# Fp4 feed-forward stage: moving VectorE's first gating product ahead of the rounding of the previous gated tile

## The reference, cut to what matters

```
x = x + ffn(layernorm(x))
gate = fp4_linear(n, w_gate);  up = fp4_linear(n, w_up)     # 256 -> 704
h = silu(gate) * up
out = fp4_linear(h, w_down)                                 # 704 -> 256
fp4_linear(a, w): both a and w are rounded to a 4-bit grid, block by block of 16,
                  with scale = max|block| / 6 and 1/scale applied before the rounding
```

## Time and profile before

| | |
|---|---|
| median of 3 runs | 2474.6 us (2470.22 to 2474.79) |
| profiled execution, its own time | 2467.79 us |
| its span, first to last instruction | 2466.0 us |
| mean granted TensorE clock | 0.976 of full speed |
| PE busy | 2354.4 us, 95% |
| DVE busy | 1782.3 us, 72% |
| ACT busy | 1293.4 us, 52% |
| POOL busy | 702.0 us, 28% |
| fp4 stage in the span | from about 380 to 886 us |

### The profile page before, as it was taken

The page is one execution under the profiler, slowest core; times in us unless marked ns, Lnnn a source line. Parts: engine busy times, 40 slices in busy tenths (PEclk is TensorE's granted clock), DMA queues, the critical chain, the costliest instruction groups (busy, mean ns, idle before and its releaser), DMA issues.

```text
span 2466.0 us, 43761 instructions
## 1 busy us (share of the span) xinstructions
PE 2354.4 (95%) x16024; PEld 2179.2 (88%) x16024; DVE 1782.3 (72%) x3323; ACT 1293.4 (52%) x2027; POOL 702.0 (28%) x468
## 2 busy tenths in 40 slices
PE   7999997999999969999999999998999999999999
PEld 6999996999999958898898898987988998899998
DVE  5776777999999857557467566555887877877774
ACT  4445444444444326456456455455666665666554
POOL 1110112555444422312213123033334442311110
PEclk9999998999999989999999999987999999999999
DMA  5000000000000000000000000011000010000001
GB/s 185 0 0 0 0 1 20 1 0 0 0 0 1 1 18 1 18 9 9 17 9 9 17 9 9 17 48 48 18 26 17 17 51 29 9 24 20 26 26 35
DMA packets 43258, 45.68 MB, mean 19 GB/s; under 512 B 3120, under 2 KB 41904, under 8 KB 43184
## 3 DMA queue, kind: packets, MB, share of 16 engines
q1 hardware_dynamic: 43184, 44.69, 5.5%
HBM read 27.90 MB, written 16.78 MB: 18 GB/s over the span
## 4 chain that ended last, share of the span: by engine, by line
PE 53%; DVE 5%; issue 3%; ACT 2%; POOL 1%; DVEq 0%; ACTq 0%; POOLq 0%
PE m_ps_z L1891 13%; PE p_ps_a L1673 5%; PE p_ps_feat L279 4%; PE p_ps_a L1730 4%; PE p_ps_feat L281 3%; PE p_ps_feat L280 3%; PE m_ps_wide L279 3%; PE m_ps_wide L281 3%; PE m_ps_wide L280 3%; PE p_ps_a L1611 2%; PE p_ps_turn L1717 2%; PE m_ps_wide L1869 1%; PE m_ps_n L1852 1%; PE m_ps_wide L1870 1%; PE m_ps_z L1897 1%
## 5 line engine op out<-in xcount | busy, mean ns | idle before, releaser
L1983 DVE TENSOR_TENSOR m_a_lo<-m_a,m_a_hi 128x512 fp32r<-128x512 f32 x256 | 202.1, 806 | 144.1 <-ACT m_a_hi L1943 140.4
L1891 PE MATMUL m_ps_z<-m_w_hi,m_a_hi 128*128 128x256 f32 x1024 | 290.7, 284 | 1.6 <-DVE m_a_lo L1983 0.9
L1891 PE MATMUL m_ps_z<-m_w_hi,m_a_lo 128*128 128x256 f32 x1024 | 288.0, 281 | 0.0
L1891 PEld LDWEIGHTS m_ps_z<-m_w_hi,m_a_hi 128*128 128x128 f32 x1024 | 192.3, 188 | 13.6 <-DVE d_w_lo L2500 1.9
L1891 PEld LDWEIGHTS m_ps_z<-m_w_hi,m_a_lo 128*128 128x128 f32 x1024 | 192.7, 188 | 0.0
L1939 ACT ACTIVATE m_a<-m_ps_wide,d_b,d_w_gain 128x512 f32<-128x512 f32 x128 | 100.0, 781 | 135.5 <-PE m_ps_wide L281 131.4
L1356 POOL TENSOR_TENSOR p_kf<-p_kf,p_k_shift 128x1024 f32<-128x1024 f32 x64 | 119.5, 1905 | 155.4 <-DVE p_k_shift L1491 155.4
L1891 PE MATMUL m_ps_z<-d_w_lo,m_a_hi 128*128 128x256 f32 x512 | 144.7, 283 | 0.0
L1891 PE MATMUL m_ps_z<-m_w_lo,m_a_hi 128*128 128x256 f32 x512 | 143.6, 280 | 0.0
L1673 PE MATMUL p_ps_a<-p_ctx_pair,p_kf 128*128 128x34 f32 x1024 | 130.0, 285 | 0.0
L1673 PEld LDWEIGHTS p_ps_a<-p_ctx_pair,p_kf 128*128 128x128 f32 x1024 | 129.5, 205 | 0.4
(11 more groups left out here) (371 smaller groups left out, 8106.2 us busy)
## 6 DMA issues: line engine op xcount, KB each, us to landing
residual<-in_x SPq DMA_DIRECT2D x8, 1024.0 KB, 11.8
attn<-p_attn SPq DMA_DIRECT2D x32, 256.0 KB, 2.1
m_attn<-attn SPq DMA_DIRECT2D x16, 512.0 KB, 3.8
out<-residual SPq DMA_DIRECT2D x16, 512.0 KB, 2.9
raw_weights<-in_d_q SPq DMA_DIRECT2D x2, 1024.0 KB, 7.1
m_attn<-in_d_scale SPq DMA_DIRECT2D x3, 512.0 KB, 4.3
raw_weights<-in_m_w1T SPq DMA_DIRECT2D x1, 1024.0 KB, 4.8
raw_weights<-in_m_w2T SPq DMA_DIRECT2D x1, 1024.0 KB, 7.9
```

The lines of the kernel that those rows point to most:

```text
L1891: mm = pe.matmul(z, a, w[:, f, :], start=(f == 0 and k == 0 and j % 2 == 0), stop=(f == FC - 1 and k == 2), skip_group_check=True)
L1983: dve.tensor_tensor(self.a2[1][:, f, :], self.a[f % RING][:, :], self.a2[0][:, f, :].bitcast(F32), ALU.subtract).then_inc(self.a_lo, 1)
```

## The change

In VectorE's order of a step, `multiply(0)` of pair s - 5 stands ahead of `round_h` of pair s - 6 and no longer behind it. Both are DVE phases; nothing is added or removed, no other engine's order changes, and the orders of steps 5 and 6 stay as they are (step 6 already has `multiply(0)` ahead of `round_h`).

```diff
-            pipeline(dve, N, [(8, add_down), (4, split_n), (7, split_h(0)), (3, round_n), (6, round_h), (5, multiply(0)),
+            pipeline(dve, N, [(8, add_down), (4, split_n), (7, split_h(0)), (3, round_n), (5, multiply(0)), (6, round_h),
                               (7, split_h(1)), (2, scales_n), (5, multiply(1)), (5, scales_h)], SLOTS,
                      fill={5: [(4, split_n), (3, round_n), (5, lambda t, s: last_statistics()), (5, multiply(0)), (2, scales_n),
                                (5, multiply(1)), (5, scales_h)],
                            6: [(4, split_n), (3, round_n), (5, multiply(0)), (6, round_h), (2, scales_n), (5, multiply(1)), (5, scales_h)]},
```

## The result

Ten runs of each: 2484.32 us median after (2479.1 to 2488.5) against 2470.78 before (2461.72 to 2474.96), 13.5 us more. The ratio on record is 1.0063, 95% interval 1.0048 to 1.0077, or 15.6 us slower (11.9 to 19.0); the quotient of the two medians, 1.0055, lies within that interval. The forecast was 13.7 us slower.

What follows compares the result with a forecast made beforehand. VectorE's queue was taken to set the step. Ordinary steps +11.3, loop turns +4.0, step 7 +0.14 and steps 34 to 36 -1.7 gave +13.7: 2474.6 + 13.7 = 2488 us, 8-in-10 range 2481 to 2495.

Steps and rivals of the forecast that it cites:

- round_h starts 0.54 later: VectorE, ordinary step: multiply(0) ahead costs round_h 0.80 less the waiting there, making the next step 0.54 us later.
- The dispatch of multiply(0): VectorE behind round_n: handing over multiply(0) might cost up to 0.34 us more in the loop's 18 steps, +6.
- L182 ends 2.72 after round_h: VectorE's L182 is held until GpSimd's restore_h ends, 2.70 to 2.73 us after round_h; its hold grows to 1.2.
- The loop's turns cost 0.79: Steps 15, 18, 21, 24, 27 have no wait ahead of round_h: 0.79 us each, 4.0 us together.
- Step 7: round_h 0.57 us later, but multiply(1)'s wait for TensorE takes up 0.43, leaving +0.14 us.
- The sum up to step 33: Steps 7 to 33: 11.3 us from 21 ordinary steps, 4.0 from five loop turns, 0.14 from step 7.
- The last steps: Steps 34 to 36 have no L182; TensorE's waits for multiply(0) of 0.60, 0.35, 0.78 vanish: -1.7 us.
- TensorE follows: VectorE's queue sets the step; TensorE's idle time moves to turn_n and turn_h(1), growing from 0.58 to about 1.1 us.
- VectorE's own waits: VectorE waits only 0.17 us for ScalarE's f_h_magic ahead of round_h and 0.26 for its reciprocal ahead of multiply(1).
- TensorE sets the step: Rival: with its wait for multiply(0) gone, the step falls to TensorE's busy 13.98, giving 2455 us; chance 2%.

Runs made afterwards that it cites:

- The run with steps 34 to 36 alone: Kernel before, old order kept except that steps 34 to 36 take the changed order; ratio to before 0.9984 (0.9974 to 0.9993).
- the fastest version: Changed kernel with scales_n split in VectorE's order: maxima, then multiply(1), then the rest with L182; ratio to before 0.9932 (0.9918 to 0.9945).
- the half restore_h: Changed kernel with restore_h cut to the first 704 of 1408 columns, for measuring alone; ratio to before 1.0049 (1.0032 to 1.0066).
- multiply(1) first: Changed kernel with multiply(1) moved ahead of scales_n in VectorE's order of a step; ratio to before 1.0071 (1.0054 to 1.0087).

## Why the prediction was right

The direction and the mechanism were right, and so was the size, though two terms of the sum erred and what happened behind step 37 made up for it. Step by step:

- *round_h starts 0.54 later.* Per step the changed kernel has 15.08 against 14.55: 0.53. The dispatch of multiply(0), for which I kept up to 0.34 in reserve, costs nothing in the loop either (0.07 to 0.09 early in every step).
- *L182 ends 2.72 after round_h.* 2.70 to 2.73 in all 28 steps after. That GpSimd is the cause was argued from two kinds of step; the runs without restore_h, with half of it, and with scales_n moved show it.
- *The loop's turns cost 0.79.* Their steps are 15.40 to 15.47, the loop's others 15.16; before both were some 14.64. So 0.77 and 0.52.
- *Step 7.* 0.14 foreseen; multiply(1) is at 439.12 and not 438.84, of which 0.13 was there in step 6 already: 0.15.
- *The sum up to step 33.* multiply(1) of step 33 starts at 833.96 and no longer at 818.76; less the 0.13 that is 15.07, where I had 15.44. The terms were 0.01 to 0.02 a step too high.
- *The last steps.* -1.7 foreseen, -2.4 measured (step 37's round_h comes 12.83 later, less 0.13, where step 33 was 15.07 late). The term was too small: I had added up the three waits as the old rows show them. A likely reason, not tested, is that without the first wait TensorE comes earlier into the next two steps than those rows have it. The run with steps 34 to 36 alone has the same 2.4, so all of it arises within them.
- *TensorE follows.* Its two new waits sum to 0.9 where I had said that its idle time grows to 1.1.
- *VectorE's own waits.* I named two. There is a third in the kernel before, 0.15 for its own reciprocal ahead of add_down. It is the same in the changed kernel, so the difference stands.

Up to round_h of step 37 the stage is thus 12.8 us longer in the traces. It ends 14.1 later: its last products start at 886.60 after 3.54 of idle time (2.24 before), the first of them takes 0.58 in place of 0.39, and the granted clock from 886.0 to 899.3 is 0.75, in the like stretch before (873 to 886) 0.87. More of that stretch than before is at TensorE's lower level, 1.2 GHz. The layers behind the stage take 1582.6 in place of 1579.8 us. I have not followed these 2.8 us to a cause; their code is the same in all eleven kernels, and there they take from 1578.9 to 1583.9, so that 2.8 is within what comes and goes without the change. They make up the rest of the two spans' difference of 16.9.

So it is in part luck that 13.7 lies so near the 13.5 of the medians. What the sum covers came to 12.7 (15.07 less 2.4); the 1.3 of the last products, for which it has no term, and the scatter of the layers behind lie on top.

Of the rivals, "TensorE sets the step" came true only where the hold is filled or gone, after the early multiply(0): there the step is 14.06 and 14.05, as against the 13.98 named for it. The Trainium skill ("SBUF — State Buffer", section "SBUF: two separate sides") says that VectorE in a two-port mode, or with two SBUF inputs while GpSimd's instruction reads SBUF, shares one port pair with GpSimd, and that whoever starts first has it for the whole instruction while the other is blocked. The traces agree for L199, which has two SBUF inputs and was held by divide_h, and for L182, which was held by restore_h or restore_n; that L182 runs in a two-port mode no row shows. The page's figure of about 115 ns is for work of GpSimd that waits for VectorE. No run here measures that direction. In this one a held L182 ended 0.02 to 0.05 us behind the recorded end of GpSimd's instruction, in every kernel here.

## What to carry to other kernels

A long duration of a tiny instruction can be a wait that no idle column shows; look whether a GpSimd instruction ends with it. Before moving work on VectorE, ask which stretch of its queue lies beside such a hold: here work inside cost nothing, and work moved in front cost its whole length less the waiting that it took up. And a wait that is removed from the engine with the larger busy share gained nothing while the other one's round trip stayed; with the hold filled again, the same move went from 0.63% slower than the kernel before to 0.68% faster.

## What the runs showed of the hardware that I had not expected

An instruction of VectorE that is already held gets its turn between two GpSimd instructions that follow each other directly (L182 ends at 818.14, with restore_n starting at 818.06 and lasting 1.09; where L182 did not stand waiting, restore_n takes 1.06). One that comes 0.06 us after the second has started waits for all of it (809.94 against 809.88). L183, the next TENSOR_SCALAR behind a held L182, gets through with it: it starts at 818.06 and takes its usual 0.17, beside a restore_n that is recorded as running from 818.06. So what decides is not the recorded overlap alone. In one place, step 7 of the fastest version, L182 was not held and L183 (here L935) came 0.03 behind the start of restore_n; it took 1.07. So a shift of some tenths can move a hold by a whole GpSimd instruction, as the half restore_h and multiply(1) first both showed.
